# Two 64-column projections of a recurrent block, placed in the two column halves of the TensorE array

## The reference

```python
xn = layernorm(x)                                   # no gain, no bias
x_norm = layernorm(xn) * ln_in_g + ln_in_b
x_norm = x_norm + depthwise_conv3(x_norm) + conv_b  # over time
gate, input_gate = split(x_norm @ gate_w.T + gate_b)
Bm = (x_norm * sigmoid(input_gate)) @ B_w.T + B_b   # 512 -> 64
Cm = x_norm @ C_w.T + C_b                           # 512 -> 64
for t in range(2048):                               # state s of 64 numbers per batch row
    s = layernorm(s @ expm(dt_A * A) + Bm[t]) * ln_st_g + ln_st_b
    ys[t] = Cm[t] * s
ssm = (ys @ D_w.T + D_b) * sigmoid(gate)
g = silu(xn @ W.T + b + (xn @ V_r) @ C.T)
out = x + ssm * g
```

## Time and profile before

| what | value |
|---|---|
| median of the runs | 2557.05 us |
| the profiled execution's own time | 2557.63 us |
| its span (first to last instruction) | 2555.8 us |
| PE busy | 2474.0 us, 97% of the span |
| DVE busy | 2201.8 us, 86% |
| POOL busy | 1275.3 us, 50% |
| ACT busy | 1006.8 us, 39% |
| mean granted TensorE clock | 0.988 of full speed |

### The profile page before, as it was taken

One profiled execution on the slowest core, in us unless ns is written; L12 is line 12 of the kernel. 1 busy time (PEld: TensorE's weight loads), 2 busy tenths in 40 slices (PEclk: granted clock), 3 DMA queues, 4 the chain that ended last, 5 costly groups with the idle time before them and its releaser, 6 DMA issues.

```text
span 2555.8 us, 42423 instructions
## 1 busy us (share of the span) xinstructions
PE 2474.0 (97%) x10001; PEld 1301.3 (51%) x10001; DVE 2201.8 (86%) x10937; ACT 1006.8 (39%) x1834; POOL 1275.3 (50%) x2485
## 2 busy tenths in 40 slices
PE   6899999999999999999999999999999999999986
PEld 3455555555555555555555555555555555555543
DVE  4688898888898888899888898888899888889876
ACT  3434344434334444334444344444344443334310
POOL 2355555455555455555455555455555455555442
PEclk8999999999999999999999999999999999999997
DMA  3111121121121122121122121122111122112112
GB/s 109 24 42 41 40 57 47 50 59 43 39 57 47 50 58 48 39 53 48 48 58 55 36 49 49 46 58 58 37 46 49 50 55 59 42 40 53 30 37 52
DMA packets 99798, 125.19 MB, mean 49 GB/s; under 512 B 32159, under 2 KB 48735, under 8 KB 99552
## 3 DMA queue, kind: packets, MB, share of 16 engines
q1 hardware_dynamic: 98912, 121.43, 19.4%
q10 hardware_dynamic: 640, 1.05, 0.2%
HBM read 71.96 MB, written 33.55 MB: 41 GB/s over the span
## 4 chain that ended last, share of the span: by engine, by line
PE 66%; DVE 15%; POOL 13%; issue 4%; ACT 0%; DMA 0%; DVEq 0%; POOLq 0%; ACTq 0%; SPq 0%
PE bank L986 17%; POOL dw L345 13%; PE bank L977 13%; PE bank L1019 8%; PE bank L969 7%; PE bank L1020 6%; DVE wq L752 6%; PE bank L996 4%; DVE dw L777 4%; DVE dw L763 4%; PE bank L1012 3%; PE bank L949 2%; PE bank L1003 2%; PE bank L959 2%; PE bank L926 1%
## 5 line engine op out<-in xcount | busy, mean ns | idle before, releaser
L345 POOL TENSOR_TENSOR dw<-q,minus_half 8x1 f32<-8x1 f32 x2048 | 1103.4, 539 | 1189.7 <-DVE wq L752 1158.7
L1019 PEld LDWEIGHTS bank<-Mscan,wT 128*65 128x65 f32 x2046 | 219.8, 136 | 670.4 <-issue 665.3
L977 PE MATMUL bank<-xnorm,gateT 128*128 128x512 f32 x1024 | 508.1, 595 | 0.0
L752 DVE SCALAR_TENSOR_TENSOR wq<-dw 8x65 f32<-8x65 f32 x2048 | 443.6, 217 | 70.5
L986 PE MATMUL bank<-xnorm,gateT 128*128 128x512 f32 x1024 | 500.9, 596 | 1.1 <-issue 1.1
L969 PE MATMUL bank<-xnT,WT 128*128 128x512 f32 x1024 | 495.2, 594 | 0.0
L1019 PE MATMUL bank<-Mscan,wT 128*65 128x128 f32 x2046 | 407.7, 281 | 36.9 <-DVE wT L780 24.6
L1020 PE MATMUL bank<-Mscan,wT 128*65 128x128 f32 x2046 | 392.9, 274 | 0.0
L777 DVE SCALAR_TENSOR_TENSOR dw<-dw 8x64 f32<-8x64 f32 x1024 | 279.8, 273 | 112.6 <-POOL dw L345 80.2
L767 DVE SCALAR_TENSOR_TENSOR dw<-bank,dw 8x128 f32<-8x128 f32 x1024 | 343.1, 335 | 24.8 <-PE bank L1020 22.4
L763 DVE SCALAR_TENSOR_TENSOR dw<-dw 8x64 f32<-8x64 f32 x1024 | 281.1, 275 | 90.8 <-POOL dw L345 82.5
(11 more groups left out here) (140 smaller groups left out, 2740.5 us busy)
## 6 DMA issues: line engine op xcount, KB each, us to landing
xc<-in_x SPq DMA_DIRECT2D x264, 128.0 KB, 2.8
out<-o SPq DMA_DIRECT2D x256, 128.0 KB, 2.4
xa<-in_x SPq DMA_DIRECT2D x248, 128.0 KB, 2.7
dw<-dtok SPq DMA_DIRECT2D x128, 96.0 KB
wtok<-dw SPq DMA_DIRECT2D x128, 33.0 KB
gateT<-in_gateT SPq DMA_DIRECT2D x1, 2048.0 KB
xa<-in_x ACTq DMA_DIRECT2D x8, 128.0 KB, 4.1
WT<-in_WT SPq DMA_DIRECT2D x1, 1024.0 KB, 6.0
```

The costliest lines, as they stand in the source:

```text
L345: nc.gpsimd.tensor_tensor(dw[0:B, t, CR:CR + 1], q[:], minus_half[0:B, 0:1], ALU.pow).then_inc(s["r_ready"], 1)
L752: V.scalar_tensor_tensor(out=wq[:], in0=w_eps, scalar=1.0 / S, in1=w_eps, op0=ALU.mult, op1=ALU.mult, accum_out=q[:]).then_inc(s["q_ready" ...
L977: ins = mm(mbank["gate", m][:], gateT[:, k, P * m:P * m + P], xnorm[p][:, k, :], start=(k == 0), stop=(k == KH - 1))
L1019: mm(scanP[0:WIDE, 0:2 * S], wT[:, 0:WIDE], Mscan[:, 0, :], start=True, stop=False)
```

## The change

B's and C's weights lose their padding: `BT` and `CwT` have 64 columns. B's projection writes partitions 0 to 63 of its bank, C's writes partitions 64 to 127 of another bank, so that the two stand in the two column halves of the array. Both are issued at the same four places (`PE_B`, now 41 to 44), B's product first, then C's; C's own places at 60 to 63 are gone. Around them other places move: the input gate leaves step 34 free and ends at 40, the gate goes from 44-59 to 45-60, the four `fill_d` go to 48, 51, 54, 57. C's bias gets a tile on partitions 64 to 127, with one more load. `copy_c` follows `copy_dT` on ScalarE; the second `copy_dtok` goes behind `normalise_z`. The waits for B's DMA leave the even step and stand at the end of steps 15, 31, 47 and 63. LayerNorm's 13 operations are reordered, with the eight that `normalise_z` needs first, and the waits follow that. In the start-up the pieces of chunk 0 get new places; C's projection of chunk 0 goes into the squarings, and `normalise_z(2)` goes ahead of `copy_c(0, 0)`.

```diff
     + [("ssm", m, "C", "bceb"[m]) for m in range(KH)] + [("ig", m, "A", "decd"[m]) for m in range(KH)] \
-    + [("b", 0, "A", "e")] + [("gate", m, "F", "abca"[m]) for m in range(KH)] + [("c", 0, "A", "b")]
+    + [("b", 0, "A", "e"), ("c", 0, "A", "c")] + [("gate", m, "F", "abca"[m]) for m in range(KH)]
...
-PE_IG = range(24, 40)
+PE_IG = tuple(range(24, 34)) + tuple(range(35, 41))
 PE_O = range(30, 46)
-PE_B = range(40, 44)
-PE_GATE = range(44, 60)
-PE_D = (46, 48, 50, 52)
-PE_C = range(60, 64)
+PE_B = range(41, 45)
+PE_GATE = range(45, 61)
+PE_D = (48, 51, 54, 57)
...
-V_XG = (29, 30, 33, 34, 37, 38, 41, 42)
-V_ADD = (35, 36, 39, 40, 43, 44, 47, 48)
-V_G = (49, 50, 53, 54, 57, 58, 61, 62)
+V_XG = (29, 30, 33, 34, 38, 39, 42, 43)
+V_ADD = (35, 36, 40, 41, 44, 45, 47, 48)
+V_G = (50, 51, 54, 55, 58, 59, 62, 63)
...
-PE_WPRIME = (2, 3, 6, 7)
-DVE_WPRIME = (3, 4, 7, 8)
-PE_Z0 = (4, 4, 5, 5)
-DVE_CONV = (7, 8, 9, 10)
-PE_IG0 = (11, 11, 12, 12, 13, 13, 14, 14, 15, 15, 16, 16, 17, 17, 18, 18)
+PE_Z0 = (2, 2, 3, 3)
+PE_WPRIME = (4, 5, 10, 11)
+DVE_WPRIME = (9, 10, 12, 13)
+DVE_CONV = (4, 5, 6, 7)
+PE_IG0 = (8, 8, 9, 9, 10, 10, 11, 11, 12, 12, 13, 13, 14, 14, 15, 15)
...
+PE_B0 = (14, 16, 17, 18)
+PE_C0 = (17, 18, 19, 19)
...
-        BT = sb("BT", [P, KH, P])
-        CwT = sb("CwT", [P, KH, P])
+        BT = sb("BT", [P, KH, S])
+        CwT = sb("CwT", [P, KH, S])
+        c_bias = sb("c_bias", [P, 1])
...
-                a_(cT[p][:], mbank["c", 0][0:S, :], ACT.Identity, bias=sm("C_b"), scale=0.5).then_inc(s["cT_done"], 1)
+                a_(cT[p][:], mbank["c", 0][S:P, :], ACT.Identity, bias=c_bias[S:P, :], scale=0.5).then_inc(s["cT_done"], 1)
...
             copy_dtok(0, 1)
+            normalise_z(2)
             copy_c(0, 0)
-            normalise_z(2)
...
-                if t % QT == 0:
-                    wait_for(dve, D_IN[t // QT], 16, i, 16)
+                if i == 0 and t == 0:
+                    wait_for(dve, D_IN[0], 16, i, 16)
...
+                if t % QT == QT - 1:
+                    of, q = divmod(i * NQ + t // QT + 1, NQ)
+                    if of < NC:
+                        wait_for(dve, D_IN[q], 16, of, 16)
...
-                ins = mm(mbank["b", 0][:], BT[:, k, :], xg[:, k, :], start=(k == 0), stop=(k == KH - 1))
+                ins = mm(mbank["b", 0][0:S, :], BT[:, k, :], xg[:, k, :], start=(k == 0), stop=(k == KH - 1))
...
-                ins = mm(mbank["c", 0][:], CwT[:, k, :], xnorm[p][:, k, :],
+                ins = mm(mbank["c", 0][S:P, :], CwT[:, k, :], xnorm[p][:, k, :],
                          start=(k == 0), stop=(k == KH - 1))
...
                         if t in PE_B:
                             b_proj(i + 1, PE_B.index(t), i, middle)
+                            c_proj(i + 1, PE_B.index(t), 1 - p, i, middle)
                         if t in PE_D:
                             fill_d(i + 1, PE_D.index(t), i, middle)
-                        if t in PE_C:
-                            c_proj(i + 1, PE_C.index(t), 1 - p, i, middle)
```

More of the change, by code:

```diff
@@ L82, with build @@
 PE_HALO = (0, 0, 1, 1)
-PE_WPRIME = (2, 3, 6, 7)
-DVE_WPRIME = (3, 4, 7, 8)
-PE_Z0 = (4, 4, 5, 5)
-DVE_CONV = (7, 8, 9, 10)
-PE_IG0 = (11, 11, 12, 12, 13, 13, 14, 14, 15, 15, 16, 16, 17, 17, 18, 18)
[L88 to L93, removed]
+PE_Z0 = (2, 2, 3, 3)
[3 more added lines that the diff above has]
+PE_IG0 = (8, 8, 9, 9, 10, 10, 11, 11, 12, 12, 13, 13, 14, 14, 15, 15)
+PE_X0 = (10, 10, 12, 12)
+DVE_XG0 = (11, 13, 15, 17)
+DVE_STATS2 = (14, 15, 16, 17)
+PE_B0 = (14, 16, 17, 18)
+PE_C0 = (17, 18, 19, 19)
+def build(nc, x, ident_d, gateT_d, WT_d, VT_d, CrT_d, BT_d, CwT_d, DT_d, vec_d, small_d, Bb_d, C_bias_d, out):
     with ExitStack() as ctx:
@@ L212, in wait_for, with wait_ln @@
             eng.wait_ge(s[name], v)
+        def wait_ln(eng, n, k):
+            if n >= 0:
+                wait_for(eng, "ln_done", LN_OPS, n, k - (LN_OPS - LN_Z if n > 0 else 0))
         def hold(eng):
@@ L242, in load_x @@
                     sp.dma_start(dst[p0:p0 + CT, b // BJ, :], x[b, bass.ds(c * CT, CT), :]).then_inc(s[name], 16)
-            for dst, src in [(small[:], small_d), (ident[:], ident_d), (vec[:], vec_d), (Bb[:], Bb_d)]:
+            for dst, src in [(small[:], small_d), (ident[:], ident_d), (vec[:], vec_d), (Bb[:], Bb_d),
+                             (c_bias[S:P, :], C_bias_d)]:
                 sp.dma_start(dst, src).then_inc(s["consts"], 16)
@@ L257, in _ @@
             sp.dma_start(gateT[:], by_rows(gateT_d)).then_inc(s["gate_in"], 16)
-            for dst, src in [(CwT[:, :, 0:S], by_rows(CwT_d)), (DT[0:WIDE, :], DT_d)]:
+            for dst, src in [(CwT[:], by_rows(CwT_d)), (DT[0:WIDE, :], DT_d)]:
                 sp.dma_start(dst, src).then_inc(s["gate_in"], 16)
@@ L360, in ln_op @@
                     wait_for(pool, "xn_done", NJ, n - 1, 0)
[L361 to L362 removed]
+                wait_ln(pool, n, k)
+                if k == 3:
                     wait_for(pool, "z_done", NJ, n, 0)
@@ L369, in ln_op @@
                     lambda: g.tensor_scalar(nm, m0, scale[0], None, ALU.mult),
+                    lambda: g.tensor_scalar(both, var, scale[1] * (1.0 + EPS), EPS * EPS, ALU.mult, ALU.add),
                     lambda: g.tensor_scalar(a, var, scale[1], EPS, ALU.mult, ALU.add),
-                    lambda: g.tensor_scalar(both, var, scale[1] * (1.0 + EPS), EPS * EPS, ALU.mult, ALU.add),
+                    lambda: half_power(both, rr, 0),
+                    lambda: half_power(both, rr, 1),
+                    lambda: half_power(both, rr, 2),
+                    lambda: half_power(both, rr, 3),
+                    lambda: g.tensor_tensor(bz, nm, rr, ALU.mult),
                     lambda: half_power(a, r1, 0),
@@ L385, in _ @@
             for n in range(3):
-                for k in range(LN_OPS):
+                for k in range(LN_OPS if n else LN_Z):
                     ln_op(n, k)
@@ L597, in iteration @@
                     copy_dT(i + 1)
+                    copy_c(i + 1, 1 - p)
                 if F:
@@ L609, in iteration @@
                     normalise_z(i + 3)
+                if A:
+                    copy_dtok(i + 1, 1)
                 if F:
                     gate_tanh(i, 3)
-                if A:
-                    copy_c(i + 1, 1 - p)
             iteration(0, 0, "ASF")
@@ L839, in _ @@
                         else:
-                            ins = V.scalar_tensor_tensor(out=BT[:, :, 0:S], in0=BT[:, :, 0:S], scalar=0.5,
+                            ins = V.scalar_tensor_tensor(out=BT[:], in0=BT[:], scalar=0.5,
                                                          in1=btmp[:].unsqueeze(2).to_broadcast([P, KH, S]),
@@ L855, in _ @@
                     bn_stats(2, DVE_STATS2.index(n), 1)
+                if n == DVE_STATS2[-1]:
+                    aggregate(2)
                 if n in DVE_XG0:
@@ L864, in _ @@
             assert done[0] == SETUP_M
[L866 to L869, removed]
             dve.wait_ge(s["pe_setup"], SQ_END + 1)
@@ L1060, in _ @@
                         fill_x(0, k, -1, False)
[L1062 to L1066, removed]
+                for k in range(KH):
+                    if PE_B0[k] == n:
+                        if k == 0:
+                            pe.wait_ge(s["bt_steps"], 3)
+                        b_proj(0, k, -1, False)
+                for k in range(KH):
+                    if PE_C0[k] == n:
+                        if k == 0:
+                            pe.wait_ge(s["wprime_done"], KH)
+                        c_proj(0, k, 0, -1, False)
             pe.wait_ge(s["dve_setup"], SETUP_M)
@@ L1084, in _ @@
                 fill_d(0, q, -1, False)
-            pe.wait_ge(s["wprime_done"], KH)
-            for k in range(KH):
-                c_proj(0, k, 0, -1, False)
             pe.wait_ge(s["dve_setup"], SETUP_END)
@@ L1137 @@
 LN_OPS = 13
+LN_Z = 8
 SETUP_VEC = 7
@@ L1165 @@
         "VT": a["L0_ffn_V_r"].T, "CrT": a["L0_ffn_C"].T, "BT": at["B_w"].T, "CwT": at["C_w"].T,
-        "DT": np.concatenate([at["D_w"].T, at["D_b"][None, :]]), "vec": vec, "small": small, "Bb": at["B_b"].reshape(1, S),
+        "DT": np.concatenate([at["D_w"].T, at["D_b"][None, :]]), "vec": vec, "small": small, "Bb": at["B_b"].reshape(1, S), "C_bias": at["C_b"].reshape(S, 1),
     }
```

36 lines of the change are left out of this document (14 added, 22 removed).

## The result

The changed kernel takes 2595.78 us (median of four runs, 2591.38 to 2598.88), against 2557.27 for the kernel before beside it: ratio 1.0147, 95% interval 1.0133 to 1.0161. It is slower, by 38 us. I had forecast slower, 2635 us with a range from 2575 to 2695: the sign is right and the time lies in the range, but the change is only half of the 78 us that I gave it. The term for the overlap was half too large (1.29 us instead of 0.86), and a rival that I had left out of the sum came true and added 23.5 us, which hid a part of the error. That the time lies in the range is luck: without those 23.5 us it would be some 2572.

A forecast was written before the change was run, and what follows sets the result against it. It took a tie of recurrence and TensorE as the bound. Stalls of 2.98 less 0.32 us a chunk, over 31 iterations, gave +82.5; start-up -4; from 2557.6 that made 2636, or 2635 against the median, range 2575 to 2695.

The forecast's parts named there:

- The tie of recurrence and TensorE: Main loop: recurrence runs at its own pace, 1.18 us a step; TensorE keeps up only because its pieces fit two steps.
- the rule of the prediction: Look-ahead before an even step: stalls the recurrence if over 0.52 us after the power with a vector piece, 0.65 without.
- The overlap term: B and C products at steps 41 to 44: only second B and first C overlap, 1.29 us a pair.
- my lower bound: B and C pair at steps 41 to 44: a whole product beside the other, 0.86 us.
- The cost of dividing: Each B and C pair at steps 41 to 44: array goes into column halves and out, 0.35 us.
- The clock: Emptied steps 61 to 63: granted clock may fall, 1 to 2.6 us each, 31 to 80 in all; 3 in 10.
- The other places: Rest of the loop: step 54's stall goes, -0.2 us; waits for B's DMA give -0.12; together -0.32 a chunk.
- The start-up: Iteration 0 and before: step 2's wait shrinks by 3.6 us, first step's time unchanged; sum -4 us.
- the whole products overlap: Rival for pairs at 41 to 44: pair 1.21 us, +25 us in all, 2582; chance 0.12.

The follow-up runs named there:

- e2_same_half: Changed kernel with C's projection written to partitions 0 to 63 too, the same column half as B's; 2705.8 us, ratio 1.0560 to the kernel before.
- f2: Changed kernel with its four B and C pairs joined two and two, at steps 42 and 44; 2610.11 us, ratio 1.0197 to the kernel before.
- e1: Changed kernel plus one dummy product at each of steps 61, 62 and 63; 2577.49 us, ratio 1.0062 to the kernel before.
- e3: Changed kernel with both projections in one half and B's and C's weights padded to 128 columns; 2657.45 us, ratio 1.0378 to the kernel before.

## Why the prediction was wrong, step by step

- **The tie of recurrence and TensorE, and lateness as what counts: right.** With the measured price of a pair, 1.15, the rule of the prediction gives stalls of 0.03, 0.60, 0.18, 0.05 and 0.16; measured are 0.04, 0.60, 0.21, 0.05 and 0.14. For prices of 1.72 and 2.00 it held to a few hundredths too. Two figures beside it were off without effect: an undisturbed step is 1.184 us and not 1.18, so that the delays of the kernel before are some 24 us and not 30, and by the rule itself the pair from which a stall appears is at 0.94 and not at 0.98.
- **The overlap term: the step that failed.** "The pair is four MATMULs, B, B, C, C, of 0.43 each", from which I took 1.29. That rested on a false reading, which also stands in the part on the kernel: that a float32 product is two MATMUL instructions in the program. The kernel calls one matmul for each product, and the built program has one instruction for it (128 for C's projection, against 256 records); the trace shows each as two records. So B and C are direct neighbours, and their first records start together and then their second ones. In place of 1.29 the columns take 0.86 (1.15 for the pair, less 0.29 for the way), my lower bound, which I had given 0.12 with the cost of dividing and 0.13 without it. In the earlier trace rows the 256 records for 128 products could not tell these readings apart; the calls in the kernel could have. The Trainium skill (TensorE: Matmul & The Clock Gate, Part 3, packing small matmuls) has distinct column tiles run at once; e2_same_half against the change bears that out, 2.00 against 1.15 us a pair.
- **The cost of dividing: right in kind, 0.35 forecast, 0.28 to 0.29 measured.** The row that I took it from had 64x64 blocks; why it was dearer there is not shown. That it is paid for each way in and out and not for each pair is shown by f2. Together both terms made 1.64 of what was 1.15: stalls of 2.98 instead of 1.04 us a chunk, which makes 1.94 x 31 = 60 us too much.
- **The clock: rival, 3 in 10, left out of the sum.** It fell 22 times in iterations 1 to 30 and cost 23.5 us (e1). "Longer than this gap" was no reason to leave it out: the clock fell after a gap of 3.3 us. The same gap stands in every chunk, and why the clock stayed up in some is not shown. The price of a fall, 1 to 2.6 us, was right at its low end (1.07; the one fall of 6.8 us cost 2.3).
- **The other places: right.** Step 54 lost its 0.22, and of the four waits the three that I had doubted gave 0.06 each and the one at 31 nothing, -0.40 in all against -0.32.
- **The start-up: -4 forecast.** Iteration 0 became 3.3 us shorter, 2.9 of it at step 2; the first power came at 89.1 instead of 86.8. Net -1, within the bounds.
- **The sum, mended:** iteration 0 has no output transposes and showed none of the stalls at 42 to 46, so 30 chunks count and not 31: 30 x (1.04 - 0.40) + 23.5 - 1 = 42, against 38.5 between the medians. Some 3 us stay unexplained. With the clock as forecast the same sum gives 18, where e1 has 16. So the rival "the whole products overlap" (pair 1.21) was the case, with a chance of 0.12, and its 25 us stood closer to that than my 78.

## What to carry to other kernels

Where a chain of small steps and a full engine share the time, work saved on the engine is worth nothing by itself. What counts is the lateness of the one instruction that the chain waits for. So add up the engine's work for each pair of steps, and place the saving where that sum is too large. Look at what a moved piece leaves behind as well: an emptied stretch on TensorE can cost the clock of the next one. Before you argue from the order of records, count the instructions of the program.

## What the runs showed of the hardware

- Two float32 products of 128 rows by 64 columns and 512 moving columns, one in each column half, start within 0.01 us of each other, record by record (991.40 and 991.88), and cost 1.15 us together with the way in and out; in the same half they cost 2.00. Without the way that is 0.86 and 1.72.
- Going from full width to halves and back costs 0.28 to 0.29 us for each visit with one pair in it (e2 against e3, and the change), and 0.33 for one with two (2.05 - 1.72, f2).
- The granted clock fell from 1.00 to 0.50 after some 3.3 us with one look-ahead, in front of 22 chunks of 31, and stayed there 3.4 us in all of them but one; three dummy products a chunk kept it at 1.00 (e1).
- An instruction for a float32 product shows as two MATMUL records in the trace, 0.43 us apart at 512 columns and the full clock. Neighbours in different halves show as B, C, B, C, in the same half as B, B, C, C.
